# First layer, reordered TensorE queue: token transposes, value and gate projections placed between the chunk pairs of the preceding slice

## The reference

```
h = rmsnorm(x, norm1_w)
q, k, v = h @ wq * HK**-0.5, h @ wk, h @ wv
g = log_sigmoid(h @ gk_w1 @ gk_w2 + gk_b) / GATE_NORM
def step(S, inp):                      # one chunk of 64 tokens
    qc, kc, vc, gc = inp
    b = cumsum(gc); qe = qc * exp(b)
    A = (qe @ (kc * exp(-b)).T) * mask
    o = qe @ S + A @ vc
    S = exp(b_last) * S + (kc * exp(b_last - b)).T @ vc
gate = h @ wg
o = rmsnorm(o, gnorm_w) * gate * sigmoid(gate)
x = x + o @ wo                         # then a gated MLP
```

## Time and profile before

| | us |
|---|---|
| median of 3 runs | 3059.62 |
| the three runs | 3059.40, 3059.62, 3071.63 |
| span of the profiled execution | 3067.1 |
| TensorE busy in the span | 2711.5 (88%) |
| VectorE busy | 2384.6 (78%) |
| ScalarE busy | 2110.9 (69%) |
| GpSimd busy | 1973.4 (64%) |

### The profile page before, as it was taken

One profiled execution on the slowest core, in us unless ns is written; L12 is line 12 of the kernel. 1 busy time (PEld: TensorE's weight loads), 2 busy tenths in 40 slices (PEclk: granted clock), 3 DMA queues, 4 the chain that ended last, 5 costly groups with the idle time before them and its releaser, 6 DMA issues.

```text
span 3067.1 us, 58582 instructions
## 1 busy us (share of the span) xinstructions
PE 2711.5 (88%) x17318; PEld 2120.1 (69%) x17318; DVE 2384.6 (78%) x5972; ACT 2110.9 (69%) x4670; POOL 1973.4 (64%) x1697
## 2 busy tenths in 40 slices
PE   4799999998569888379799999999999999999997
PEld 2466666665469765267588788787887878878786
DVE  3466666666377589558599999998899999999896
ACT  4444454443255466346599999998999999999996
POOL 3322222214424214555399999998999999999998
PEclk7799999997889899689899999999999999999999
DMA  6355445455766544446777776767666666676673
GB/s 168 94 176 170 168 165 185 149 195 168 238 178 199 168 154 151 157 128 199 230 240 237 236 237 205 220 204 220 219 206 217 205 210 216 205 224 199 203 218 113
DMA packets 320436, 588.35 MB, mean 192 GB/s; under 512 B 47888, under 2 KB 138800, under 8 KB 319632
## 3 DMA queue, kind: packets, MB, share of 16 engines
q1 hardware_dynamic: 305776, 545.07, 57.6%
q0 software_dynamic: 14352, 39.54, 3.5%
HBM read 464.44 MB, written 124.17 MB: 192 GB/s over the span
## 4 chain that ended last, share of the span: by engine, by line
POOL 34%; issue 10%; ACT 3%; DVE 1%; PE 1%; DMA 1%; POOLq 1%; SPq 0%; ACTq 0%; DVEq 0%
POOL mm L2706 8%; POOL y L2719 7%; POOL yz L2723 7%; POOL y L2733 6%; POOL y_lo L2712 6%; ACT mt L2636 1%; DVE cv L2789 1%; DMA wi<-ssm_wi_split 1%; POOLq L2382 1%; ACT ys L2650 0%; ACT mt L2656 0%; DVE bank L2860 0%; ACT L2671 0%; POOL first L2748 0%; PE bank L64 0%
## 5 line engine op out<-in xcount | busy, mean ns | idle before, releaser
L2706 POOL TENSOR_TENSOR mm<-mt,cb 128x512 f32<-128x512 f32 x384 | 490.2, 1299 | 56.9 <-ACT mt L2656 54.9
L2636 ACT ACTIVATE mt<-a_wide,a_tok 128x128 f32<-128x128 f32 x1536 | 487.1, 389 | 3.5 <-POOL mm L2706 2.5
L2789 DVE SCALAR_TENSOR_TENSOR cv<-bank,taps,cv 128x509 f32<-128x509 f32 (+2 forms) x576 | 429.3, 745 | 13.6
L64 PE MATMUL bank<-f,wi 128*128 128x512 f32 x768 | 322.4, 420 | 14.7 <-DMA wi<-ssm_wi_split 14.6
L65 PE MATMUL bank<-f,wi 128*128 128x512 f32 x768 | 305.7, 398 | 0.0
L66 PE MATMUL bank<-f,wi 128*128 128x512 f32 x768 | 305.7, 398 | 0.0
L2723 POOL TENSOR_TENSOR yz<-y,zs 128x512 f32<-128x512 f32 x192 | 249.2, 1298 | 15.0
L2712 POOL TENSOR_TENSOR y_lo<-yz,y_hi 128x512 fp32r<-128x512 f32 x192 | 246.2, 1282 | 8.4 <-ACT y_hi L2661 6.5
L2719 POOL TENSOR_TENSOR y<-t 128x512 f32<-128x512 f32 x192 | 246.0, 1281 | 0.0
L2529 PE MATMUL bank<-mm,x_tok 128*64 128x128 f32 x3072 | 226.4, 283 | 13.1 <-POOL mm L2706 13.1
L2733 POOL TENSOR_TENSOR y<-y,ys 128x512 f32<-128x512 f32 x184 | 237.6, 1292 | 0.1
(11 more groups left out here) (476 smaller groups left out, 8067.5 us busy)
## 6 DMA issues: line engine op xcount, KB each, us to landing
wi<-ssm_wi_split SPq DMA_DIRECT2D x192, 512.0 KB
a_wide<-a_scratch SPq DMA_DIRECT2D x192, 512.0 KB
l_fw<-ffn_split SPq DMA_DIRECT2D x72, 768.0 KB
ea<-ea_scratch SPq DMA_DIRECT2D x384, 128.0 KB
wo<-ssm_wo_split SPq DMA_DIRECT2D x192, 256.0 KB, 4.1
sorted_scratch<-ex_zeros SPq DMA_DIRECT2D x96, 130.5 KB
ssm_wi_split<-l_s_out SPq DMA_DIRECT2D x24, 512.0 KB
ey_x<-sorted_scratch SPq DMA_DIRECT2D x94, 130.5 KB
```

The lines of the kernel that those rows point to most:

```text
L64: pe.matmul(out, wh, xh, start=first, stop=False)
L2636: i = act.activation(mt[:, h, chunk(j)], a_wide[:, g % R, h, chunk(j)], ACT.Relu, bias=a_tok[:, s * NJ + j, 2 * t + h:2 * t + h + 1], scal ...
L2706: pl.tensor_tensor(mm[:, :, ts], mt[:, :, ts], cb[:, js, :].rearrange("p j t -> p (j t)") .unsqueeze(1).broadcast_to([P, 2, TS // 2]), ALU ...
L2789: dve.scalar_tensor_tensor(cv[:, a:TS], bank[:, X, 0:TS - a], taps[:, t, k:k + 1], cv[:, a:TS], ALU.mult, ALU.add).then_inc(ph["tap"], 1)
```

## The change

Three lists are written in another order; no instruction is added or taken away. TensorE: the transposes of slice a stand after the first chunk pair, its values after the second, its gate after the third, and the fourth pair stands last, right before `head_squares`. ScalarE: the copy of the transposes, the copy of the values and the tanh of the gate stand earlier; the tanh stands before the second split copy and before the squares. Of the three table loads in this part (L866, L871, L880) the first now stands ahead of the tanh and so ahead of the squares; the other two stay behind them. VectorE: `first_low` stands before the second pair, and `gate_product` stands right after the last state update, ahead of `second_low` and `scale_out`.

```diff
@@ -723,21 +723,21 @@
                         ranks()
                     if has(c):
                         outputs(c, 0)
-                        scores(c, 1)
-                        outputs(c, 1)
-                        scores(c, 2)
                     if has(a):
                         token_rows(a)
                     if has(c):
-                        outputs(c, 2)
-                        scores(c, 3)
+                        scores(c, 1)
+                        outputs(c, 1)
                     if has(a):
                         values(a)
                     if has(c):
-                        outputs(c, 3)
+                        scores(c, 2)
+                        outputs(c, 2)
                     if has(a):
                         output_gate(a)
                     if has(c):
+                        scores(c, 3)
+                        outputs(c, 3)
                         head_squares(c)
                     if has(a):
                         query_key(a)
@@ -836,24 +836,30 @@
                         act.activation(rt["ex"][:, :, 0:E0], rt["sh"][:, :, 0:E0], ACT.Exp).then_inc(ph["rexp"], 1)
                         done(act, "e1", a)
                         act.activation(g_l[:], g_l[:], ACT.Ln, bias=1.0).then_inc(ph["l1"], 1)
+                    if has(a):
+                        done(act, "xt", a)
+                        done(act, "yms", a - 2)
+                        act.activation(xo[:].rearrange("p k t -> p (k t)"),
+                                       bank[:, 4:6, :].rearrange("p j d -> p (j d)"), ACT.Copy).then_inc(ph["x_tok"], 1)
                     if has(f) and f < G - 1:
                         second_log(f)
                         exp_of(r2[:], "r2", f)
                     high(split_of(k, 0))
                     if has(a):
-                        done(act, "xt", a)
-                        done(act, "yms", a - 2)
-                        act.activation(xo[:].rearrange("p k t -> p (k t)"),
-                                       bank[:, 4:6, :].rearrange("p j d -> p (j d)"), ACT.Copy).then_inc(ph["x_tok"], 1)
+                        done(act, "v_ps", a)
+                        done(act, "o_ps", (a - 2) * NC0 + NC0 - 1)
+                        act.activation(v[:, a % 2].rearrange("p j d -> p (j d)"),
+                                       bank[:, 4:6, :].rearrange("p j d -> p (j d)"), ACT.Copy).then_inc(ph["v"], 1)
                         done(act, "cum", a)
                         done(act, "ke", a - 1)
                         act.activation(enb[:], cum[:], ACT.Exp, scale=-1.0 / GNORM).then_inc(ph["enb"], 1)
                         done(act, "rest", a)
                         act.activation(rest[:], rest[:], ACT.Exp, scale=1.0 / GNORM).then_inc(ph["el"], 1)
-                        done(act, "v_ps", a)
-                        done(act, "o_ps", (a - 2) * NC0 + NC0 - 1)
-                        act.activation(v[:, a % 2].rearrange("p j d -> p (j d)"),
-                                       bank[:, 4:6, :].rearrange("p j d -> p (j d)"), ACT.Copy).then_inc(ph["v"], 1)
+                    if has(a):
+                        act.preload_act_table(ACT.Tanh)
+                        done(act, "gate_ps", a)
+                        done(act, "og", a - 2)
+                        act.activation(sgate[:, a % 2], bank[:, 4:6, :], ACT.Tanh, scale=0.5).then_inc(ph["tgate"], 1)
                     if has(f) and f < G - 1:
                         features_high(f)
                     high(split_of(k, 1))
@@ -862,11 +868,6 @@
                         done(act, "onorm", c - 1, 2)
                         for gr in range(2):
                             act.activation(by_chunk(hs[:, gr, :]), heads_out(gr), ACT.Square).then_inc(ph["sqo"], 1)
-                    if has(a):
-                        act.preload_act_table(ACT.Tanh)
-                        done(act, "gate_ps", a)
-                        done(act, "og", a - 2)
-                        act.activation(sgate[:, a % 2], bank[:, 4:6, :], ACT.Tanh, scale=0.5).then_inc(ph["tgate"], 1)
                     if has(c):
                         act.preload_act_table_set("natural_log_exp_and_others")
                         done(act, "hms", c)
@@ -1226,10 +1227,10 @@
                     if has(a):
                         route(a)
                         gate_min(a)
+                    if has(a):
+                        first_low(a)
                     if has(c):
                         core(c, 1)
-                    if has(a):
-                        first_low(a)
                     if has(f) and f < G - 1:
                         second_norm(f)
                     scale_out(split_of(k, 0))
@@ -1240,13 +1241,13 @@
                     if has(c):
                         core(c, 3)
                         advance(c, NC0 - 1)
+                    if has(a):
+                        gate_product(a)
                     if has(f) and f < G - 1:
                         second_low(f)
                     if a == G:
                         place()
                     scale_out(split_of(k, 1))
-                    if has(a):
-                        gate_product(a)
                     if has(c):
                         out_norm(c)
                     if has(f):
```

## The result

| | before | after |
|---|---|---|
| median, us (4 runs each) | 3060.15 | 3094.72 |
| lowest to highest, us | 3059.40 to 3071.63 | 3090.39 to 3103.67 |
| ratio after / before, 95% interval | | 1.0116 [1.0090, 1.0143] |
| span of the profiled execution | 3067.1 | 3088.6 |
| its time | 3071.63 | 3090.39 |

The change makes the kernel 34.6 us slower. The prediction was 3062.6 us, with 3080 as the upper end of its range. The two profiled executions lie only 18.8 us apart: that of before was the slowest of its four runs (11.5 us over the median), that of after the fastest of its four (4.3 us under it). 18.8 + 11.5 + 4.3 = 34.6. The traces therefore show about half of the loss, and the rest has to be asked of medians.

What follows compares the result with a forecast made beforehand. TensorE was taken to bound the kernel, by waits and its clock. Six full beats at +0.85 us (3.8 - 2.05 - 0.9) make 5.1, less 2 for small waits: +3, 3062.6 us; range 3042 to 3080.

Steps and rivals of the forecast that it cites:

- beats 0 and 1: The partial beats: a later split copy in beat 0 and a changed chain in beat 1 were to cancel.
- the waits of the full beats: TensorE's waits in beats 2 to 7: +3.8 and -2.05 us a beat, -2 us for the small waits between pairs.
- the clock's gain: Full beats: half of a 5.3 us loss won (-2.7), +1.8 for a fall after the new wait: -0.9 us a beat.
- wait before L639: Before the head squares: without the gate as cover, 4.1 us of open wait in place of 0.31, +3.8 a beat.
- wait before the second MLP step: Table load and tanh leave the chain to L1185, so the whole 2.05 us wait goes in each full beat.
- waits between and in the pairs: About 4 us in beats 2 to 4; half taken as won, -2 us for the run, between -4 and +3.
- the forecast of under 0.3 us: Sign in the changed profile: the 2.05 us wait before the second MLP step falls under 0.3 us.
- over the 1 us inside the pairs: Sign of being wrong: a new wait of over 1 us inside the chunk pairs.
- the 4 to 9 that were forecast: Sign in beat 5: the half-clock stretch lasts 4 to 9 us in place of 13.
- The terms +1.4 and -1.3: Beat 0: +1.4 us for later split copies; beat 1: -1.3 us, shorter chain to the attention output less unhidden squares.
- rival B: Full beats: wait before L639 paid, clock wins nothing; +3.55 us a beat, six times 21.3, 3081 to 3084 us; chance 0.17.
- its sign for the place where it decides: It decides from the point where the cold stretch in the pairs stays near 13 us.

Runs made afterwards that it cites:

- e2: New order of the three lists in beats 0 and 1 only, the old order elsewhere: 3075.71 us, 1.0040 of the kernel before.
- e3: Changed kernel with ScalarE's second split copy moved behind the squares, their logarithm and exponential: 3081.76 us, 1.0061 of the kernel before.
- e14: Order of e1, with the transposes between the second pair's scores and outputs: 3081.12 us, 1.0071 of the kernel before.
- e4: As e3, with the transposes also between the second pair's scores and outputs: 3081.90 us, 1.0048 of the kernel before.
- e5: Kernel before plus matmuls with unread results in TensorE's idle time ahead of the rank matmuls of beats 1 and 2: 3057.23 us, 0.9992 of before.
- e9: New order in beat 0 only, the old order in all other beats: 3066.53 us, 1.0019 of the kernel before.
- e10: New order in beat 1 only, the old order in all other beats: 3065.95 us, 1.0017 of the kernel before.
- e13: As e2, plus unread matmuls in TensorE's idle time ahead of the rank matmuls of beats 1 and 2: 3063.66 us, 1.0006 of the kernel before.
- e1: New order of the three lists in beats 2 to 7 only, the old order in beats 0 and 1: 3083.16 us, 1.0062 of the kernel before.
- e6: Changed kernel plus unread matmuls in TensorE's idle time ahead of the rank matmuls of beats 1 and 2: 3095.41 us, 1.0125 of the kernel before.
- e7: Gate last again, transposes between the second pair's scores and outputs, values between the third's, in all beats: 3048.65 us, 0.9962 of the kernel before.
- e11: Changed kernel with only the gate's move undone on all three lists, tanh and product included: 3075.61 us, 1.0043 of the kernel before.
- e12: Order of e7 in beats 2 to 7 only, the old order in beats 0 and 1: 3049.06 us, 0.9971 of the kernel before.

## Why the prediction was wrong

It forecast +3 us and +34.6 were measured. Three of its terms make up most of the difference: beats 0 and 1, priced at nothing, cost 12 us; the waits of the full beats, priced at 8.5, come to 19.1; and the clock's gain of 5.4 is not there. By its own terms, for beats 2 to 7 unless said otherwise:

| term of the prediction | predicted | measured |
|---|---|---|
| wait before L639 | 6 x 3.8 = +22.8 | +21.3 |
| wait before the second MLP step | 6 x -2.05 = -12.3 | -10.5, all waits for L1185 -9.7 |
| waits between and in the pairs | -2 | +1.2 |
| wait before L601 | not priced | +6.6 |
| idle in all (with small others) | +8.5 | +19.1 |
| clock | 6 x -0.9 = -5.4 | -6.5 between these two executions, +5.3 between the means of several |
| beats 0 and 1 | 0 | +12 (e2) |

**Right: the new wait.** L639 waits for L870 for 3.90 us (3.71 in beat 4) in all six beats, VectorE's L1220 right before, and the tanh has ended before the last pair's outputs. e3 showed the copy behind the scaling to be the piece of this path that can be taken away.

**Mis-sized: the wait that goes.** Before the second MLP step the 2.05 us have gone altogether in beats 4 and 5, and to 0.33 to 0.52 us in the other four; the forecast of under 0.3 us is met in two beats of six. Waits for the read-out before later steps stay (0.61 us before the third in beat 5, where it was 0.52). At the second step it is 10.5 us in place of 12.3, and later steps wait 0.8 more, so in all 2.6 us less than predicted.

**Failed: what stands on VectorE when the transposes are moved up.** The prediction counted what is queued behind the moved pieces and not what they themselves wait for. They take banks 4 and 5 after the decay gate's read-out, L1135, and VectorE reaches it only behind the router's rows. It priced this at nothing, and missed 6.6 us in the trace, though the trace of before showed 1.6 us of it in beat 5. The same lateness turned the -2 us for the pairs into +1.2: the mask (L1018) is now waited for 16 times, for 1.22 and 1.25 us in beats 4 and 7. That is over the 1 us inside the pairs which the prediction had named as a sign that it was wrong. e14 shows that these two hang together: take the wait before L601 away, and in two beats of three most of it stands before the second outputs. In the time this step is worth little by itself (e4, e14).

**Failed: the clock's gain, whose base was one execution.** Between the two traces the term looks right. The cold stretch between the pairs shrank as hoped, from 13 to 3.2 us in beat 5 (under the 4 to 9 that were forecast), and after the new wait 4.0 us of work on average are done at half clock, where 3.6 were taken. But the stretch of 13 us that was to be cut belongs to some executions of the old order and not to all. In beat 5 before and e5 have 13.6 us of half clock; e2, e9, e10 and e13, with the same order there, have 7 to 10. In e10 it is two short stretches:

```profile
425.60:428.80 3.20, 3.20 (x17) 1.00 (x16) 3.13 (x6) 1.56 (x4) 2.50 (x3) 0.50 0.52 144
439.20:442.40 3.20, 3.20 (x12) 1.41 (x9) 2.95 (x6) 1.26 (x2) 0.00 (x0) 0.50 1.06 376
```

Busy time over the full beats was 491.3 (after), 503.1 (e1) and 492.7 (e6) with the new order, mean 495.7; in kernels with the old order in these beats it was 497.8, 496.1 (e2), 492.2 (e5), 485.2 (e9), 488.1 (e10) and 482.9 (e13), mean 490.4. The ranges overlap, and the gain of 5.4 us that the prediction counted is not there. Idle time was 57.5 to 62.1 (mean 59.9) against 39.3 to 47.0 (mean 42.5). Together that is 23 us, inside e1's 13 to 25. That the clock term came out at -6.5 between the two traces is luck.

**Failed, and the largest term: beats 0 and 1.** The terms +1.4 and -1.3 were to cancel. Each beat costs 5 to 6 us (e9, e10), 12 together (e2). The prediction had priced only instructions and waits there, and these are the smaller part: in the profiles idle time grows by 3 us on average, busy time by 12. It did not ask what a shift does to the clock in beats where TensorE is idle for 40 of 111 us: full clock came back at 104.8 us in place of 76.0. The move behind it is the gate's, since with the gate last (e7, e11) the first beats are busy for 73.8 to 74.9 us.

The sum: full beats 19 and first beats 12 make 31 of 35 us; the other 4 lie within the intervals. The outcome is nearest to rival B, the wait paid and the clock winning nothing: its 21 to 24 us are within what e1, the full beats alone, measured (13 to 25). That it fits is partly luck: B had no wait for L601 and nothing for the first beats, and its sign for the place where it decides did not come, since in the profiled beat 5 the stretch in the pairs did shrink.

Still open: why the unread matmuls, which bring e2 back by 0.34%, bring the whole changed kernel nothing (e6), though its profile has beats 0 and 1 in 116.9 us in place of 127.9. As long as this is open, that the first beats' loss is clock is shown for e2 alone. Open too are what keeps the clock down until 104.8 us when the gate is moved, and which of the two moves inside the pairs carries e12.

## What to carry to other kernels

When a block is moved up in a queue, follow its own waits backward through every engine's list, not only what stands behind it: a bank that was free two pairs later may not be read out yet. A block that covers another engine's chain (here the gate, over scaling, copy and squares) is worth what it covers, and its removal also costs the clock that falls in the new wait. Cut both traces at the same marks into idle and busy time of the bounding engine; when the count of instructions is the same, one column is the waits, the other the clock. Neither is exact: over six executions with the same order in these beats the waits lay within 8 us and the clock's column within 15, so that a term of 5 us read from one pair of traces says little. Look at the beats where the engine is half idle, too: here they cost 12 us of the 35.

## What was unexpected of the hardware

- The same 2744 or 2745 matmuls in the same order took from 482.9 to 497.8 us of busy time (old order, six profiles) and from 491.3 to 503.1 (new order, three), while the idle time stayed within 7.7 and 4.6 us. A single profile says little on a clock term of 5 us.
- A VectorE operation on 56 columns (L1072) took 0.22 us in three full beats and 1.99, 2.05 and 2.37 us in the other three. The three long ones began while GpSimd's L968 (1024 columns, 2.4 us) was running and ended within 0.1 us of its end; the short ones did not overlap it. The same holds for before (2.00, 2.03 and 2.39 us), e1 and e14: in the four profiles it took 2.0 us or more twelve times, always in beats 3, 5 and 6. The waits of about 2 us before L601 are in exactly these beats. Beat 5, GpSimd:

```profile
442.17 2.37 POOL L968 TENSOR_TENSOR l_base<-l_x,l_xn 128x1024 f32<-128x1024 f32 x1 [17.85 <-DMA acc_scratch<-l_base]
```

- Full clock came back about 6.8 us after the fall in the wait of 3.7 to 3.9 us, in each of the six full beats. Where matmuls followed without a gap in e12, it came back after 3.2 us in beat 5, but after about 6.8 us in beats 3 and 6.
